# Relation layers of a graph network: fewer and coarser waits of TensorE in the loop over pairs of groups

## What is computed

```
def _fast_rgcn_layer(x, src, tgt, edge_type, W_r, root_r, bias_r):
    seg = tgt * R + edge_type
    msg = x[src]
    agg = segment_sum(msg, seg, num_segments=N * R).reshape(N, R, d)
    cnt = segment_sum(ones, seg, num_segments=N * R).reshape(N, R, 1)
    agg = agg / clip(cnt, 1.0, None)
    out = einsum('nrd,rdo->no', agg, W_r)
    return out + x @ root_r + bias_r
```

## Times and profile before

| | us |
|---|---|
| median of 3 runs | 3733.86 (3727.67 to 3737.41) |
| the profiled execution | 3700.42 |
| its span, first to last instruction | 3698.7 |
| relation layers within it | about 1604 to 3694 |

### The profile page before, as it was taken

The page is one execution under the profiler, slowest core; times in us unless marked ns, Lnnn a source line. Parts: engine busy times, 40 slices in busy tenths (PEclk is TensorE's granted clock), DMA queues, the critical chain, the costliest instruction groups (busy, mean ns, idle before and its releaser), DMA issues.

```text
span 3698.7 us, 82678 instructions
## 1 busy us (share of the span) xinstructions
PE 2784.9 (75%) x25480; PEld 1786.5 (48%) x25481; DVE 2202.9 (60%) x7982; ACT 1375.2 (37%) x3073; POOL 1211.2 (33%) x1250
## 2 busy tenths in 40 slices
PE   3211666667689999958888888788888878888887
PEld 1110333333355565535555556555555555555555
DVE  6666888888664534325555555455555555555555
ACT  0322777777632222023333332333333333333332
POOL 1002000000000000015555554455555545555554
PEclk9555888888899999979999999899999989999999
DMA  0002000001111101154444444444444444444443
GB/s 23 0 8 58 37 35 35 35 35 37 58 43 30 56 17 49 56 154 124 121 122 123 127 122 114 118 122 128 121 122 122 121 119 122 124 124 125 122 122 85
DMA packets 197029, 315.97 MB, mean 85 GB/s; under 512 B 36705, under 2 KB 131276, under 8 KB 196924
## 3 DMA queue, kind: packets, MB, share of 16 engines
q1 hardware_dynamic: 155932, 226.92, 20.8%
q0 software_dynamic: 40992, 87.70, 8.4%
HBM read 269.54 MB, written 44.95 MB: 85 GB/s over the span
## 4 chain that ended last, share of the span: by engine, by line
PE 23%; issue 12%; DMA 11%; DVE 4%; another core or an unknown queue 3%; POOL 2%; DVEq 1%; ACT 1%; POOLq 0%; SPq 0%; ACTq 0%
DMA arena<-pair,arena 11%; PE psum L1939 8%; PE psum L1952 6%; PE psum L1963 4%; PE psum L1916 3%; POOL arena L1856 2%; DVE arena L2128 2%; PE psum L1929 1%; DVE arena L2124 1%; DVE arena L2134 1%; DVE arena L2164 1%; PE psum L1890 1%; DVEq L2157 0%; DVEq L2164 0%
## 5 line engine op out<-in xcount | busy, mean ns | idle before, releaser
L1856 POOL DMA_INDIRECT arena<-pair,arena x1212 | 1159.3, 956 | 910.3 <-issue 335.2
L2134 DVE SCALAR_TENSOR_TENSOR arena<-psum,arena,work 128x304 f32<-128x304 f32 x606 | 313.2, 518 | 766.7 <-DMA h<-h 564.0
L1952 PE MATMUL psum<-arena 128*128 128x304 f16 x3939 | 580.0, 294 | 49.2 <-issue 46.4
L2067 ACT ACTIVATE arena<-psum 128x1024 f16<-128x1024 f32 x303 | 310.2, 1024 | 780.8 <-DMA h<-h 311.8
L1939 PE MATMUL psum<-arena 128*128 128x304 f16 x2424 | 380.4, 297 | 182.6 <-DMA arena<-pair,arena 159.2
L1092 PE MATMUL psum<-arena,h 128*128 128x512 f16 x1750 | 481.8, 381 | 19.9 <-DMA h<-h 19.9
L2128 DVE TENSOR_SCALAR arena<-arena 128x304 f16<-128x304 f16 x2121 | 487.1, 300 | 0.0
L1952 PEld LDWEIGHTS psum<-arena 128*128 128x128 f16 x3939 | 360.6, 98 | 242.1 <-issue 129.6
L1963 PE MATMUL psum<-arena 128*128 128x152 f32 (+1 forms) x2496 | 383.6, 299 | 25.7 <-DVE arena L2134 24.5
L1093 PE MATMUL psum<-arena,h 128*128 128x128 f16 x1750 | 384.7, 220 | 0.0
L1916 PE MATMUL psum<-arena 128*32 128x256 f16 x7272 | 328.5, 279 | 63.6 <-issue 57.6
(11 more groups left out here) (258 smaller groups left out, 3430.2 us busy)
## 6 DMA issues: line engine op xcount, KB each, us to landing
work<-winv SPq DMA_DIRECT2D x303, 304.0 KB
arena<-pull SPq DMA_DIRECT2D x303, 224.0 KB
pull<-rows SPq DMA_DIRECT2D x101, 224.0 KB
arena<-pair,arena POOLq DMA_INDIRECT x1212
h<-work SPq DMA_DIRECT2D x12, 640.0 KB, 3.3
h<-h POOLq DMA_DIRECT2D x12, 640.0 KB, 7.5
pair<-arena SPq DMA_DIRECT2D x12, 256.0 KB
x_pad<-arena SPq DMA_DIRECT2D x1, 1600.0 KB, 7.3
```

Of the source, the lines that this page charges most:

```text
L1856: e.indirect_dma_start(out=t.msg[:, j, k].rearrange("p h f -> p (h f)"), out_offset=None, in_=d[f"pair_{l}"].rearrange("n h f -> n (h f)") ...
L1952: m = e.matmul(p.psum[:, 1, 0:KEYS], t.smsg[:, j % 2, tile, half, :], t.soh[:, j % 2, tile, :], start=(tile == 0 and half == 0), stop=(til ...
L2067: e.activation(t.smsg[:, q, 0:4].rearrange("p k h f -> p (k h f)"), p.psum[:, GATHER:GATHER + 2, :].rearrange("p b n -> p (b n)"), ACT.Cop ...
L2134: e.scalar_tensor_tensor(t.agg[h % 2][:, :, k % BATCH, :], p.psum[:, k % 2, 0:KEYS].rearrange("p (r w) -> p r w", r=REL), t.back[:, l:l + ...
```

## The change

In `quad`, the wait for the first copy (at c = 0) becomes a wait for all four copies of the fill before, and the wait at c = 4 goes. In `gathered`, the wait for the pair's four one-hots becomes a wait for all eleven. In `filled`, the waits for copies (at tile 0 and tile 4) and for one-hots go; the one for copies stays for the last pair of a layer alone, which no later `quad` follows. In `apply`, the wait for the adds of the batch before goes. Matmuls, activations, vector work and DMAs stay the same, in the same order.

```
@@ -1909,8 +1909,6 @@
                 slot = j % G_AHEAD
                 if c == 0:
                     e.wait_ge(s_pl[slot], turn * (16 * TP // G_AHEAD) + 16 * (l * uses(slot) + j // G_AHEAD + 1))
-                    e.wait_ge(s_gv, at * TAKES + 1)
-                elif c == 4:
                     e.wait_ge(s_gv, at * TAKES + TAKES)
                 for b in range(4 * c, 4 * c + 4):
                     m = e.matmul(p.psum[CAP * (b % 4):CAP * (b % 4) + CAP, GATHER + c // 2, c % 2 * 2 * RF:(c % 2 + 1) * 2 * RF],
@@ -1933,7 +1931,7 @@
             def gathered(turn, j, tile):
                 if tile == 0:
                     e.wait_ge(s_got[j % TP], turn * (16 * GT) + got(l, j % TP, j // TP))
-                    e.wait_ge(s_oh, turn * (TP * HOT_PAIR) + ((l * PAIRS + j) * HOT_PAIR + GT))
+                    e.wait_ge(s_oh, turn * (TP * HOT_PAIR) + ((l * PAIRS + j) * HOT_PAIR + HOT_PAIR))
                     e.wait_ge(s_ev, turn * TURN + (l * NG + 2 * j + EV0 - 1))
                 for half in range(2):
                     m = e.matmul(p.psum[:, 0, 0:KEYS], t.msg[:, j % TP, tile, half, :], t.oh[:, j % 2, tile, :],
@@ -1941,13 +1939,11 @@
                 if tile == GT - 1:
                     m.then_inc(s_mm, 1)
 
-            def filled(turn, j, tile):
+            def filled(turn, j, tile, last_fill):
                 if tile == 0:
-                    e.wait_ge(s_gv, turn * (TAKES * TP) + (TAKES * (l * PAIRS + j + 1) + 1))
-                    e.wait_ge(s_oh, turn * (TP * HOT_PAIR) + ((l * PAIRS + j) * HOT_PAIR + HOT_PAIR))
+                    if last_fill:
+                        e.wait_ge(s_gv, turn * (TAKES * TP) + TAKES * (l * PAIRS + j + 2))
                     e.wait_ge(s_ev, turn * TURN + (l * NG + 2 * j + EV0))
-                elif tile == 4:
-                    e.wait_ge(s_gv, turn * (TAKES * TP) + TAKES * (l * PAIRS + j + 2))
                 for half in range(2 if tile < SLOT_TILES - 1 else 1):
                     m = e.matmul(p.psum[:, 1, 0:KEYS], t.smsg[:, j % 2, tile, half, :], t.soh[:, j % 2, tile, :],
                                  start=(tile == 0 and half == 0), stop=(tile == SLOT_TILES - 1))
@@ -1957,7 +1953,6 @@
             def apply(turn, h, groups, part):
                 if part == 0:
                     e.wait_ge(s_ev, turn * TURN + (EV0 + l * NG + h * BATCH + groups))
-                    e.wait_ge(s_ad, turn * TURN + (AD0 + l * NG + (h - 1) * BATCH))
                 n = groups * RWIN
                 for r in range(part * REL // PARTS, (part + 1) * REL // PARTS):
                     m = e.matmul(p.psum[:, OUT + h, 0:n], t.wr[:, r, :],
@@ -1980,7 +1975,7 @@
                             quad(turn, j + 1, c)
                         spares(j + 1, PIECES * (j - first))
                     for tile in range(SLOT_TILES):
-                        filled(turn, j, tile)
+                        filled(turn, j, tile, not fills)
 
             if l:
                 e.wait_ge(s_lo, 7 * l)
```

## The result

The changed kernel takes 3759.25 us (median of 5 runs, 3756.36 to 3776.79), the kernel before 3730.72 (5 runs beside it, 3727.67 to 3737.41): ratio 1.0082, 95% interval 1.0057 to 1.0107. It is 28.5 us slower. The chance of slower was 0.25.

The account below looks back on a forecast made before the run. GpSimd's runs of four gathers and TensorE's late signals were taken to set the pace; about 1 us gained at layer starts and ends against 0.8 lost left about 0, so 3734 us, range 3704 to 3778.

Parts of the forecast that it names:

- likeliest case: Whole kernel: no change, 3734 us, with a range of its own from 3722 to 3748; chance 0.52.
- Second quads: 0.13 us a pair, from a gap of 0.16: TensorE's second quads: without their wait, idle ahead falls from 0.16 to 0.03 us, gaining 0.13 a pair.
- `filled`, `apply`, one-hots: nothing: TensorE's `filled`, `apply` and `gathered`: waits dropped or moved to eleven one-hots change nothing; at best 0.05 us a pair.
- The quads' wait binds, and slack hides it: First quads: waiting for all four copies starts them 0.26 or 0.63 us late, but the round absorbs it.
- TensorE locks to the round with slack, and the round stays 6.5 us: TensorE's loop: `filled` ends 6.9 us after a round's signals, 1.7 us before its next quads may start; pace unchanged.
- The pace: GpSimd's gathers: still runs of four, 395 gathers of a layer taking 643 to 648 us.
- sign against the slack: GpSimd's gathers: four taking more than 6.58 us on the mean would show the copies' chain slowing the kernel.
- Once 0.8 us at the first layer's start: First layer's start: quads wait 0.82 us for copies, delaying `gathered` and GpSimd's ninth gather; plus 0.8 us, once.
- The slower rival: Added wait chains ScalarE's copies into TensorE's path: 0.45 us in each of 154 pairs, 3768 to 3803 us; chance 0.22.
- TensorE's own time as the bound: TensorE's true end sets the signals, so removed gaps count: up to 0.18 us a pair, 3679 to 3706 us; chance 0.20.
- Shifted transfers: SyncE's transfers shift against GpSimd's runs: 0.05 us a round, 15 us up or down, 3719 or 3749 us; chance 0.06.

Follow-up runs that it names:

- fourth kernel: Changed kernel with the second quads' wait for four copies put back behind the first quads' same wait: 3325.83 us, ratio 0.9988 on a quick chip.
- one-gate kernel: Changed kernel without GpSimd's wait ahead of a pair's third gather: 3311.46 us, ratio 0.9904 on a quick chip; 3734.66 us, 1.0092 on another.

## Why the prediction missed its likeliest case

Its points, in its order:

1. *Second quads: 0.13 us a pair, from a gap of 0.16.* Wrong by the whole term. The gap is 0.16 without the wait. A wait that is already met was not what filled it; the fourth kernel, which puts one back behind another, has 0.16 us there too (2504.28 in its trace) and isn't slower than its sisters (0.9988). It made no difference to the forecast, since the gain was then written off.
2. *`filled`, `apply`, one-hots: nothing.* Not refuted. The changed kernel's gap ahead of `filled` is 0.21 still, its total loss equals that of the quads' edit alone within the intervals, and on quick chips the other edits make 1.0007, 1.0013 and 0.9999. They were not timed alone on a chip on which the change costs; that stays open to some 0.3%.
3. *The quads' wait binds, and slack hides it.* It binds as said: 204 waits, 0.56 us in the median, where the two stretches had 0.26 and 0.63. And in the usual round of four gathers the slack does hide it, so that the mean hardly moves: with the quads' edit alone such a round takes 6.54 us, before 6.52. **The step that failed is the next sentence, that "TensorE locks to the round with slack, and the round stays 6.5 us".** I worked the slack out for a run of four, in which ScalarE gets the signals of both parts of the fill together, about a microsecond behind the run, and took it for all rounds. In the median round of four gathers of the changed kernel the spares end 4.8 us into the run, near its end, and a signal that is held until behind the run costs little. In 18 of the 19 places with a wait over 2 us they end 1.7 to 3.1 us into it, in 13 runs of four and five runs of five; in the 19th it is 4.1 us, in a run of six. In 16 of the 19 the first copy starts within 0.4 us of the run's start, so that it is made early, but in 18 of the 19 the second starts only 1.1 to 1.3 us after the run's end. The added wait puts the quads, and `gathered` behind them, behind that copy: 2.2 to 4.4 us at a time, 19 times. The five longest, 4.0 to 4.4 us, stand in four runs of five and in the run of six. Why TensorE comes early against a run is clear for ten of the 19 alone: five stand where GpSimd pauses after a single gather and then issues five, and five right behind runs of two, which come from an earlier such place. The trace of before could have told: in it the second copy starts over 3 us behind the spares 18 times, up to 5.4 us, where the median is 1.7.
4. *The pace.* 395 gathers of a layer took 663.9, 658.0 and 659.8 us, not 643 to 648: 6.66 to 6.72 us for four, beyond the 6.58 that the prediction gave as its sign against the slack. Some 26 us of the excess (259 runs by 0.10) is pace that the change probably did not make: two traces of the changed kernel on chips that run before in 3729 to 3731 us have 6.62 and 6.63 us for four, while the quads' edit alone and the one-gate kernel, on chips of 3704 to 3708, have 6.54 and 6.52. There is no trace of the kernel before on a chip of 3729 to 3731 us, so that is inferred. The rest is the 18 added pauses of GpSimd: with the quads' edit alone it pauses 38 us longer than before, and these gathers of the three layers take 28 us longer.
5. *Once 0.8 us at the first layer's start.* The ninth gather of the first layer comes 26.8 us after its first now, and came 25.9 before: about as said.

The slower rival named the right circle (fill, late signal, copies, quads) and put it in the wrong place. It charged 0.45 us to each of 154 ordinary pairs, 69 us, and the point from which it decides, 1.7 us more than counted. Ordinary pairs pay next to nothing (6.54 us for four against 6.52); the few in which the signal is later than the slack wait 2 to 4 us each, and the kernel loses some 30 us in all. That the range held the result was luck: its upper end was put past half of those 69 us, a sum over pairs that lose nothing, and the loss comes from others. The other two: TensorE's own time as the bound would have shown a gain with the other edits, and on the chips where TensorE is the bound (the round of 5.16 us) there is none, since the gaps stay. Shifted transfers were not tested by themselves; nothing above needs them.

On the late signal itself: by the Trainium skill ("Perfetto Trace Analysis", section "Tensor Engine Instruction (MATMUL, LD_WEIGHTS)") the semaphore is pushed once PSUM has acknowledged the bytes. On the quick chip the trace agrees, ScalarE starts 0.13 us after the modelled end. On the others it is 5.1 and 7.5 us in the two stretches above, with GpSimd's gathers running and ending first. That TensorE still works all that time is unlikely: in the stretch of the changed kernel the spares end by the model at 1830.89 and the `filled` sums behind them at 1832.68, but ScalarE acts on the first signal at 1836.00 and VectorE on the second (L2129) at 1836.05. Work that lies 1.8 us apart is signalled within 0.05 us, as if both signals had been held and let go together. The trace's own record of the spares' semaphore has its count go up at 1835.89, so it is not ScalarE that is slow to look. What holds them is not shown.

Open: why the chips differ; whether waiting for two copies costs less than for four (timed on a quick chip alone); and whether the kernel before with one gate a pair would beat both kernels on every chip. The one measured winner is the changed kernel with one gate on quick chips, 0.9904; on the others it loses 0.9% like the change.

## What to carry to other kernels

Slack worked out for the ordinary round covers the ordinary round alone. Look in the trace for the rounds of another shape (a loop's turn, a run that is longer by one, an engine that comes early), find the longest time that the signal behind an added wait has ever taken, and hold the slack against that. Here the trace of before had it: 5.4 us, where 1.7 is usual. Waiting for the last of four small steps in place of the first costs nothing while signals are prompt, and ties a queue to the slowest signal when they aren't. And an already met wait taken out of a busy queue may save nothing at all: compare the gap with one at a place that has no wait.

## What was new about the hardware

The same program takes 3330 to 3341 us on three chips and 3704 to 3731 on the others that ran it, at the same granted clock (0.918 in both traces of the quads' edit alone). Gathers take 0.95 us on both kinds, and GpSimd issues them without a pause for up to 88 in a row on a quick chip (one-gate kernel); in the quads' edit alone on a quick chip ScalarE's second copy starts within 0.7 us of the spares' end in every fill. On the other kind a signal of TensorE that falls into a run of gathers may stay out until 1 to 2 us after the run's end, up to 7.5 us late, but need not: of the 240 fills before whose spares end inside a run, 169 have their second copy start before the run's end. And in a run of eight TensorE's own weight loads come one in 0.7 to 1.4 us.

Behind a wait of 4.4 us what follows is slower too (windows of the changed kernel: stretch, us, busy time of PE, PEld, DVE, ACT and POOL with their counts, granted clock, DMA share, GB/s): sixteen quads' loads that take 0.34 us took 0.57 at 1837.10, and the granted clock in 1837.10 to 1838.50 is 0.50, the lower of the two levels (1.2 GHz), where it was 1.00 in 1828 to 1831:

```profile
1828.00:1831.00 3.00, 3.00 (x34) 2.35 (x31) 2.57 (x12) 1.02 (x1) 1.97 (x2) 1.00 0.53 183
1837.10:1838.50 1.40, 1.40 (x18) 0.74 (x19) 1.40 (x8) 0.00 (x0) 1.09 (x2) 0.50 0.42 113
```
